# Constant products on TensorE ahead of two expert layers, set-up work moved into later slots, and a re-ordered router in the last layer

## What is computed

```
x = x + _L0_attn_a_ref(_layernorm(x), W_K, W_Q, W_V, W_O)
x = x + _L0_ffn_ref(_layernorm(x), w_red, wg, w1, b1, w2, b2)
x = x + _L0_attn_b_ref(_layernorm(x), w_qkv, b_qkv, w_out, b_out)
x = x + _L0_ffn_ref(_layernorm(x), w_red, wg, w1, b1, w2, b2)

# the expert layer, per token
logits = (x @ w_red) @ wg_n.T                    # wg_n: rows of wg at unit norm, 8 experts
gates  = softmax(logits);  idx = argmax(gates);  score = gates[idx]
h      = gelu(x @ w1[idx] + b1[idx])             # 128 -> 512, exact gelu
out    = (h @ w2[idx] + b2[idx]) * score
```

## Time and profile before

| | |
|---|---|
| median of 3 executions | 1243.08 us (1242.02 to 1244.05) |
| the profiled execution | 1235.74 us |
| its span, first to last instruction | 1234.0 us |
| instructions | 24704 |
| TensorE busy, mean granted clock | 1135.5 us (92%), 0.963 |
| VectorE, ScalarE, GpSimd busy | 930.9, 808.1, 832.8 us |

### The profile page before, as it was taken

How to read it: one execution, slowest core, us unless ns; L and a number is a source line. 1 busy time by engine, 2 the same in 40 slices (tenths; PEclk the granted TensorE clock), 3 DMA queues, 4 the chain that set the end, 5 groups by cost and what they waited for, 6 DMA issues and landing times. The chain is left out here.

```text
span 1234.0 us, 24704 instructions
## 1 busy us (share of the span) xinstructions
PE 1135.5 (92%) x8010; PEld 847.9 (69%) x8010; DVE 930.9 (75%) x2054; ACT 808.1 (65%) x2248; POOL 832.8 (67%) x814
## 2 busy tenths in 40 slices
PE   6999999999999999999999999999999669687477
PEld 4776677677767776777677767767776559354377
DVE  5887878787787778778877787788787546598645
ACT  6877676767786767777777767776777346342355
POOL 3687678857786788677677757785878435585434
PEclk9999999999999999999999999999999879799579
DMA  5000810081018002700450063002004232100131
GB/s 145 27 1 1 210 49 2 6 229 35 1 35 224 2 1 58 209 1 2 117 141 1 2 176 92 1 18 52 2 1 126 86 92 67 35 1 1 56 98 50
DMA packets 72908, 75.71 MB, mean 61 GB/s; under 512 B 8487, under 2 KB 61869, under 8 KB 72784
## 3 DMA queue, kind: packets, MB, share of 16 engines
q1 hardware_dynamic: 69776, 67.80, 20.6%
q0 software_dynamic: 3008, 6.34, 1.5%
HBM read 15.34 MB, written 42.91 MB: 47 GB/s over the span
## 5 line engine op out<-in xcount | busy, mean ns | idle before, releaser
L604 DVE TENSOR_REDUCE at_nmax<-at_ps 128x1 f32<-128x512 f32 (+3 forms) x640 | 374.6, 603 | 122.0 <-PE at_ps L853 119.1
L510 POOL TENSOR_SCALAR at_prob<-at_prob,at_scale 128x512 f32<-128x512 f32 (+3 forms) x307 | 424.5, 1401 | 2.0
L850 PE MATMUL at_ps<-at_k_st,at_q_parts 128*128 128x512 f32 (+3 forms) x640 | 285.6, 446 | 4.0 <-DVE at_q_parts L663 2.0
L721 ACT ACTIVATE at_prob<-at_ps,at_nmax 128x512 f32<-128x512 f32 (+3 forms) x416 | 259.9, 631 | 43.5 <-DVE at_nmax L604 42.7
L879 PE MATMUL at_ps<-at_probT,at_v 128*64 128x256 f32 (+1 forms) x2304 | 270.1, 374 | 0.6 <-DVE at_probT L627 0.6
L734 ACT ACTIVATE at_probT<-at_ps 128x512 f32<-128x512 f32 (+1 forms) x288 | 165.2, 574 | 148.8 <-PE at_ps L864 122.6
L853 PE MATMUL at_ps<-at_k_st,at_q_parts 128*128 128x512 f32 (+3 forms) x640 | 252.2, 394 | 0.0
L627 DVE COPY at_probT<-at_ps 128x512 f32<-128x512 f32 (+1 forms) x288 | 189.1, 657 | 51.6 <-PE at_ps L864 42.8
L510 POOL TENSOR_SCALAR late<-late,at_scale 128x512 f32<-128x512 f32 (+1 forms) x168 | 226.4, 1364 | 1.6
L864 PE MATMUL at_ps<-ident,at_prob 128*128 128x128 f32 x1440 | 220.1, 273 | 5.1 <-DVE at_probT L627 4.3
L879 PEld LDWEIGHTS at_ps<-at_probT,at_v 128*64 128x64 f32 x2304 | 152.1, 136 | 102.5 <-issue 40.9
(11 more groups left out here) (241 smaller groups left out, 1488.3 us busy)
## 6 DMA issues: line engine op xcount, KB each, us to landing
slots_in<-empty SPq DMA_DIRECT2D x6, 2967.0 KB, 18.9
slots_in<-empty SPq DMA_DIRECT2D x6, 2838.0 KB, 18.4
at_q_parts<-at_q_parts SPq DMA_DIRECT2D x64, 256.0 KB, 3.5
f_xs<-slots_in SPq DMA_DIRECT2D x46, 129.0 KB
late<-in_L_ffn_w_dram SPq DMA_DIRECT2D x1, 2048.0 KB, 9.0
late<-in_L_ffn_w_dram SPq DMA_DIRECT2D x4, 512.0 KB, 6.6
rows<-in_L_attn_a_x_dram SPq DMA_DIRECT2D x4, 256.0 KB, 3.8
rows<-new_x SPq DMA_DIRECT2D x4, 256.0 KB, 3.7
```

Source lines behind the costliest of these rows:

```text
L510: pool.tensor_scalar(cols, cols, scale[:, k, u, c:c + 1], None, ALU.mult).then_inc(s_fix["pool"], 1)
L604: dve.tensor_reduce(nmax[:, q % 2, 2 * i + h, c:c + 1], bank, AX.X, ALU.max, negate=True).then_inc(s_max, 1)
L721: act.activation(prob[ROW_HOME[j]][u][:, c * BANK:c * BANK + w], ring[use_of["score", p, j, i, h, c] % RING][:, 0:w], ACT.Exp, bias=nmax[: ...
L850: pe.matmul(bank[:, 0:w], q_hi[h][:, r * P:(r + 1) * P], keys, start=True, stop=False)
```

## The change

- At the end of attention's TensorE list stand 240 products of two bf16 constants of 128x128 (`before`, `all`) into a bank that nothing reads any more. Nothing waits for them but the barrier behind them.
- TensorE's list of the first expert layer begins with 60 such products. In the last one there are 170, behind a new wait for `s_slot` (the slots are known).
- `beside` no longer stands ahead of the slots of the first expert layer. SyncE's four loads go behind its eighth slot load, VectorE's three operations ahead of the weights of slot 12, TensorE's four transposes ahead of xT of slot 14, ScalarE's copy ahead of xT of slot 16. GpSimd's part stays.
- In the last expert layer the square roots are taken twice instead of four times: chunk 0, and chunks 1 to 3 at once. VectorE takes the statistics of chunks 1 to 3 directly behind norm(0), and its order per chunk is now norm(c), find_place(c-1), choose(c). TensorE does turn(c), score_experts(c), rank(c) chunk by chunk. ScalarE copies chunk c and takes its exponential, in turn.

```diff
--- before.py
+++ after.py
@@ -906,6 +906,9 @@
                                              start=True, stop=True)
                         last.then_inc(s_vproj, 1)
 
+                for _ in range(240):
+                    pe.matmul(turn_ps[0][:, 0:P], keep["all"][:, :], keep["before"][:, :], start=True, stop=True)
+
         nc.clear_and_free_semaphores(sems)
         nc.all_engine_barrier()
 
@@ -1000,12 +1003,12 @@
 
             @block.sync
             def _(sp):
-                if beside:
-                    beside["sync"](sp)
                 sp.wait_ge(keep["s_slot"] if scattered else s_slot, 2)
                 sp.wait_ge(keep["s_scattered"] if scattered else s_scat, 16 * NT)
                 for s in range(SLOTS):
                     k = s % LOADED
+                    if beside and s == LOADED:
+                        beside["sync"](sp)
                     if s >= LOADED:
                         sp.wait_ge(s_ys, s - LOADED + 1)
                     row = sp.value_load(keep["slot_row"][0:1, s:s + 1], min_val=0, max_val=E * T + (E - 2) * P)
@@ -1053,9 +1056,12 @@
 
                 def norm(c):
                     rows = slice(TPC * c, TPC * (c + 1))
-                    dve.wait_ge(s_std, c + 1)
-                    dve.reciprocal(rstd[:, rows], rstd[:, rows]).then_inc(s_rstd, 1)
-                    dve.wait_ge(s_rstd, c + 1)
+                    if c < 2:
+
+                        dve.wait_ge(s_std, c + 1)
+                        rows = slice(TPC, NT) if c else rows
+                        dve.reciprocal(rstd[:, rows], rstd[:, rows]).then_inc(s_rstd, 1)
+                        dve.wait_ge(s_rstd, c + 1)
                     for t in tiles_of(c):
                         dve.tensor_scalar(xn[:, t, :], x[:, t, :], mv[:, t, 0:1], rstd[:, t:t + 1],
                                           ALU.subtract, ALU.mult).then_inc(s_xn, 1)
@@ -1084,30 +1090,26 @@
 
                 if not scattered:
                     statistics(0)
-                    statistics(1)
                     norm(0)
                     for c in range(1, NC):
+                        statistics(c)
+                    choose(0)
+                    for c in range(1, NC):
                         norm(c)
-                        if c + 1 < NC:
-                            statistics(c + 1)
-                        if c >= 2:
-                            find_place(c - 2)
-                        choose(c - 1)
-                    find_place(NC - 2)
-                    choose(NC - 1)
+                        find_place(c - 1)
+                        choose(c)
                     find_place(NC - 1)
 
                 count = ranks(NC - 1)[:, :, TPC:TPC + 1]
                 if not scattered:
                     find_slots(dve, link, shp, keep, count, over, small, passed, moved, slot_row, slot_e, s_slot)
-                if beside:
-                    beside["vector"](dve)
-
                 dve.wait_ge(keep["s_wall"], 16 * (2 * FCH + 2))
                 dve.wait_ge(keep["s_slot"] if scattered else s_slot, 2)
 
                 def emit(stage, s, k):
                     mine = xs[s % LOADED]
+                    if beside and (stage, s) == ("weights", LOADED + U):
+                        beside["vector"](dve)
                     if stage == "weights":
                         if s >= U:
                             dve.wait_ge(s_ys, s - U + 1)
@@ -1140,23 +1142,17 @@
                     act.activation(ex[:, TPC * c:TPC * (c + 1), :], sub[:, TPC * c:TPC * (c + 1), :], ACT.Exp).then_inc(s_ex, 1)
 
                 if not scattered:
+                    for rows in (slice(0, TPC), slice(TPC, NT)):
+                        act.wait_ge(s_aggr, rows.stop)
+                        act.activation(rstd[:, rows], mv[:, rows, 1], ACT.Sqrt, bias=keep["eps"][:, 0:1]).then_inc(s_std, 1)
                     for c in range(NC):
-                        if c == NC - 1:
-                            exponential(0)
-                        act.wait_ge(s_aggr, (c + 1) * TPC)
-                        rows = slice(c * TPC, (c + 1) * TPC)
-                        act.activation(rstd[:, rows], mv[:, rows, 1], ACT.Sqrt, bias=keep["eps"][:, 0:1]).then_inc(s_std, 1)
-                        if c:
-                            act.wait_ge(s_xnTp, c)
-                            act.activation(xnT[:, (c - 1) * BANK:c * BANK], ps[(c - 1) % 2][:, :], ACT.Copy).then_inc(s_xnT, 1)
-                    act.wait_ge(s_xnTp, NC)
-                    act.activation(xnT[:, (NC - 1) * BANK:NC * BANK], ps[(NC - 1) % 2][:, :], ACT.Copy).then_inc(s_xnT, 1)
-                    for c in range(1, NC):
+                        act.wait_ge(s_xnTp, c + 1)
+                        act.activation(xnT[:, c * BANK:(c + 1) * BANK], ps[c % 2][:, :], ACT.Copy).then_inc(s_xnT, 1)
                         exponential(c)
-                if beside:
-                    beside["scalar"](act, ps[4])
 
                 def emit(stage, s, k):
+                    if beside and (stage, s) == ("xT", LOADED + 2 * U):
+                        beside["scalar"](act, ps[6])
                     if stage == "xT":
                         act.wait_ge(s_xsTp, s + 1)
                         if s >= U:
@@ -1208,17 +1204,21 @@
                     last.then_inc(s_rank, 1)
 
                 if not scattered:
-                    turn(0)
-                    for c in range(1, NC):
+                    for c in range(NC):
                         turn(c)
-                        score_experts(c - 1)
-                        rank(c - 1)
-                    score_experts(NC - 1)
-                    rank(NC - 1)
-                if beside:
-                    pe.wait_ge(beside["tensor"](pe, ps[4]), 1)
+                        score_experts(c)
+                        rank(c)
+
+
+                if not scattered:
+                    pe.wait_ge(s_slot, 2)
+                for _ in range(60 if scattered else 170):
+                    pe.matmul(ps[6][:, 0:P], keep["all"][:, :], keep["before"][:, :], start=True, stop=True)
 
                 def emit(stage, s, k):
+
+                    if beside and (stage, s) == ("xT", LOADED + U + 2):
+                        beside["tensor"](pe, ps[6])
                     if stage == "xT":
                         pe.wait_ge(s_xs[s % LOADED], 16 * (s // LOADED + 1))
                         if s >= 2:
@@ -1305,7 +1305,6 @@
         for a in range(4):
             last = pe.transpose(bank[:, a * P:(a + 1) * P], w_nat[:, a, :], ident[:, :])
         last.then_inc(s_wTp, 1)
-        return s_wT
 
     def on_scalar(act, bank):
         act.wait_ge(s_wTp, 1)
```

## The result

The changed kernel takes 1249.59 us (median of 5, 1248.95 to 1250.46) against 1243.08: 1.0052 of before, interval 1.0041 to 1.0063. That is +6.5 us; +4.6 and 1247.7 were forecast. Two further comparisons gave 1.0053 (1.0038 to 1.0067) and 1.0048 (1.0035 to 1.0061).

The account below looks back on a forecast made before the run. Bounds: GpSimd's scatters at attention's barrier, the first expert layer's head, and the last layer's scatters and slots, with TensorE at half clock at both heads. 5.7 - 3.45 + 0.45 + 1.9 = +4.6 us, so 1247.7 us, range 1243 to 1254.5.

Parts of the forecast that it names:

- Price of one constant: On TensorE, one bf16 product of 128 columns takes 0.107 us at the low clock, 0.056 at full, its load hidden.
- Part 1: Attention's end: 240 constants make TensorE last at the barrier, which opens at 999.0 instead of 993.28, +5.7 us.
- rivals of 0.080: Stationary loads are not hidden, each constant costs 0.080 us: +8.5 us on top, 1256.2; one case in ten.
- of less than 0.041: Constants cost under 0.041 us and fit under attention's scatters, barrier stays at 993.28: -3.7 us, 1239.4; 8 in 100.
- the rival that it would not: Attention's barrier does not wait for TensorE's constants to run: sum +3.0, 1246.1 us; 12 in 100.
- Part 2: First expert layer's head: first second-weight product comes 7.95 us behind the barrier instead of 11.41, -3.45 us.
- The clock was not lost there: Rival at the first expert layer's head: clock lost between the 60 constants and first second-weight product, 1250 us; 10 in 100.
- Part 3: First expert layer's later slots: TensorE's four moved transposes cost +0.45 us, the other engines' moved set-up work 0.
- Nothing before y0 counts any more: Expert layers: TensorE has no gap from the first second-weight product on, so measuring there suffices; no size given.
- Part 4: Last layer's router: first scatter about 12.7 us behind block's begin, last scatter about +0.5, slots' table at 29.6 instead of 26.2.
- Part 5: Last layer: 170 constants behind the slots' table outlast the rows' landing, first second-weight product at 1187.15 instead of 1185.23, +1.9 us.

Follow-up runs that it names:

- e3: The changed kernel without the 170 products of the last layer, the wait for the slots' table kept: 1238.88 us, 1.0012 of before.
- e4: The changed kernel with the last layer's router order of before, constants and set-up work as changed: 1238.64 us, 1.0005 of before.
- e1: The kernel before again, no edit, for a second profile: 1237.42 us, 0.9995 of before.
- e12: The changed kernel with the router of before, 120 products instead of 240 and 100 instead of 170: 1240.73 us, 0.9968 of before.
- e10: The changed kernel again, no edit, beside a new profile of the kernel before: 1250.97 us, 1.0048 of before.
- e5: The changed kernel again, no edit: 1250.73 us, 1.0053 of before.
- e8: The changed kernel with the router of before, 90 products instead of 240 and 120 instead of 170: 1239.62 us, 0.9964 of before.
- e9: The kernel before a third time, no edit, one profile: 1242.3 us, against a median of 1244.56 among these runs.
- e11: The kernel before with GpSimd's 16 last-layer scatters held until the slots' table is there: 1254.89 us, one time, 10 over before.
- e2: The changed kernel without the 240 products at attention's end: 1240.59 us, 1.0023 of before.
- e7: The kernel before with only the linear layer's set-up work moved to later slots: 1241.27 us, 0.9981 of before.
- e6: The changed kernel with 8 columns instead of 128 in each of the 240 products: 1247.63 us, 1.0036 of before.

## Why the prediction was right, and where it was off

**Direction and size** were right: slower by more than can be told from no change, +4.6 forecast, +6.5 measured, inside the range.

**Price of one constant**, 0.107 and 0.056 us with the load hidden: right, 0.056 at the full clock. The rivals of 0.080 and of less than 0.041 are out. The Trainium skill (TensorE: Matmul & The Clock Gate, "Back-to-back issue gap") gives about 81 ns for a sustained pair of weight load and product of 128 columns; the trace does not agree, with 139 such pairs 0.056 us apart.

**Part 1**, barrier +5.7: right where results are on time, +5.6 and +6.0 (e3 and e4 against e1). The clock rose anywhere from 2.7 to 8.6 us after the products began (e12; e10), wider than the ends of 3 and 7. No barrier opened before the products had ended, and with 240 of them it opened 1.1 us behind their end, so the rival that it would not is out.

**Part 2**, y0 at 7.95 us behind the barrier: 8.04 to 8.16 (the changed kernel, e3, e4, e5, e10). The clock was not lost there with 240 products, but it was with 90 and 120 (e8, e12).

**Part 3**, +0.45 in the slots and nothing else: +0.43 and +0.44, against the first profile and e9.

**"Nothing before y0 counts any more"**, the ground on which both layers were measured at y0, does not hold where the clock rises behind y0. That cost the kernel before 1.8 us in the first expert layer (e1, e11) and 2.0 in the last (e9), and in every profile with constants in front of a layer's slots the clock was up at y0. The prediction read a profile in which it rose just ahead of y0 both times, 0.9 and 0.5 us, and so gave the constants nothing for this.

**Part 4**, first scatter at 12.7, last one +0.5, table at 29.6: 12.87, +0.3 and 30.6 where nothing is late (e2, e3). The mechanism was right; a chunk takes 5.3 to 5.4 us, not 5.1.

**Part 5** is the term that was most mis-sized. "+1.9 us" for the last layer's y0 measured +3.7 (e2: 47.2 against 43.4 to 43.6). The prediction had the products begin behind a table at 29.6 and 4.5 us of low clock; the table came 1.0 later and the low clock lasted 5.6 (e2) or 5.9 (e4), and their end moves with both: 43.0 us behind the begin in e2, where 41.2 was forecast.

With these, 5.6 - 3.4 + 0.43 + 3.7 = 6.3 us. But these are numbers of the lower level, and the +6.5 was measured at the higher one. There the division is another one, e10 against e9: barrier +6.4 (without the 1.07 of attention), y0 behind it -3.3, slots +0.44, y0 of the last layer +5.5, from there to the end -2.1, together +7.0. That the two sums are so close is in part luck: at the higher level y0 of the last layer moves 1.8 us more than at the lower one, and the -2.1 behind it has no counterpart there. In the profiles of the higher level linear attention, which the change does not touch, takes 1.2 to 1.6 us longer with the change. The clock falls near its end, before the last tiles' transposes: windows of TensorE in e9 (block over at 1144.52) and e10 (1150.73):

```profile
1142.00:1143.00 1.00, 0.63 (x5) 0.92 0.00 0
...
1146.00:1147.00 1.00, 0.00 (x0) 0.53 0.00 0
```

It fell 1.7 and 4.7 us before the end. Of the fourteen profiles six have the block at 88.2 to 88.3 us, and in these the clock fell 1.2 to 2.1 us before its end; eight have it at 89.4 to 90.2, and there it fell 4.4 to 5.0 us before. The two go together, but this was not tried by itself: no run moved the fall alone.

**Not in the prediction at all**: the two levels of the kernel before. It took 1235.74 as a typical execution and added a difference to a median 7 us higher. At the lower level the difference can only be estimated, for the whole change was not run there: +1.5 (e3) and the 3.6 of the 170, or +2.8 (e2) and the 3.6 of the 240, give 5.1 to 6.4 us. That the size is nearly the same at both levels was luck more than method.

## What to carry to other kernels

Work that only warms an engine has to end before the thing it bridges to: measure the idle time that it fills, from the same wait, at the low clock and with its start as late as the change makes it. The same 170 products gained 0.6 us behind one router and lost 3.6 behind another that gave the table 4.4 us later; and products ahead of a barrier are held against the last other engine at that barrier, here 10.7 us (13.0 in e9) for 15 to 19 us of work. Set-up work moved into a later loop, where it cost TensorE 0.44 us, gained without any of this (e7).

## What was unexpected of the hardware

- In some sets of runs results of TensorE reached the waiting engine up to 5.1 us late (3.4 to 3.9 us at attention's end, 0.65 to 5.1 in the last router) while GpSimd's indirect DMAs were under way, and were on time in the last router when these were held back (e9, e11); the same kernel is 5.3 to 6.8 us faster in a set without this (e1), under the same chip number. TensorE's own stream has gaps of about 0.5 us there (e6, e12). What makes them is open; holding the scatters removed the late results.
- 120 products that arrive with such gaps did not keep the clock: it fell 1.4 us after their end (e12), while after gap-free stretches it stayed for 4.9 us (e8) and for more than 4 us (first expert layer's end). This was seen and not tried by itself.
- The same kernel's clock rose ahead of y0 in one profile and 3.7 us behind it in another, and that alone made the 1.7 us between them (e1).
